# Nine VectorE operations of a graph network's first layer: from one chunk of edges per round to two chunks per two rounds

## The chip, the cores and the metric

The kernel runs on one core of one Trainium2 chip. The metric is the device time of one execution in microseconds, the median of several runs.

## The reference, cut to what matters

Two message-passing layers run over a graph of 3125 nodes with 160 features each (64 scalars and 32 vectors of 3 components) and 100000 edges that are sorted by their target node. The change touches the first layer alone. For every edge:

```python
msg = (rows_src[src] + rows_dst[dst])                 # 160 features: s (64) and v (32 x 3)
w1 = rbf @ W_rbf                                      # 16 -> 224 factors
m1_s = [w_ss*s*y0, w_vv0*(v . y1)/sqrt3]              # 96
m1_v = [w_sv*s*y1, w_vs*v*y0, w_vv1*cross(v,y1)/sqrt2]# 128 x 3
a = leaky(m1_s @ W_alpha) . alpha_dot                 # attention logits, 4 heads
val_s, val_v = m1_s @ Ws_val, (m1_v @ Wv_val) * sigmoid(gate)
m2 = the same tensor product of (sigmoid(val_s), val_v) with y0, y1
h = m2 @ W_vlin                                       # 160 features, stored per edge
```

Later stages take a softmax of the logits over each target's edges, sum the weighted h per target, and run the second layer.

## The kernel before, in words

**Tiling.** The edges are cut into 392 chunks of 256 (`NCH`); a chunk is two tiles (`G` = 2) of 128 edges, an edge to a partition. Four chunks are a super step (`Q`), for which one load brings indices and one the radial features. `loop_steps` writes out the first 8 rounds, then a hardware loop whose body is 8 rounds, then the last ones. A passage from one turn of that body to the next is called a seam below. Every engine runs its own list of rounds t, and semaphores of the table `LA` tie them together.

**One chunk v through the engines.**
- POOL (`gather_src`, line 657) fetches the source and target rows with four indirect DMAs, in the order source, target, source, target, into ring `gat0` (8 chunks, in tile ACC) and ring `dst_rows` (in tile TAB). It waits for `m` and `tp` of chunks 7 or 8 before, that is, until the rings' old contents are used.
- TensorE (`factors0`, line 795) multiplies the radial features into bank W1. ScalarE (`weigh0`, lines 1114 to 1118) scales them by the edge attributes into `WS0`, first half of the chunk at the end of one round, second half at the beginning of the next, and signals `ws`.
- VectorE builds the message. These are the nine operations of the change: `joined0` (line 1484), `products0` (1509), `crossed0` (1515), two in `others0` (1520, 1521), two in `rest_of_s0` (1527, 1528), two in `rest_of_v0` (1534, 1535). The last one signals `m`.
- TensorE turns the message (`t1`, line 803, into bank TR1), ScalarE copies it out (`copies`, line 1129, signals `c1`), TensorE multiplies by the attention and value weights (`e1`, lines 825 and 827, into bank E1, signals `e1`).
- VectorE takes the result: `gated` (1546), `gated_up` (1552), `summed` (1559), `scaled` (1577), `mixed_dots` (1590), `bent_sums` (1566), `mixed_rest` (1597 to 1603, signals `tp`); ScalarE squashes the gates (`squash`, 1140 and 1141) and weighs the rest (`weigh2`, 1152 and 1157).
- TensorE turns this second product (`t2`), ScalarE copies it (`c2`, line 1129), TensorE multiplies by the last weights (`hm`, lines 850 and 852, bank HP). VectorE makes the vector part (`head_products` 1613, `head_values` 1622, signals `hv`), ScalarE copies the scalar part (`scalars0`, 1167), and SyncE stores 256 rows.

**Order within a round.** It is written out by hand in each engine's `stage0`. In VectorE's round t, message operations of chunk t+1 are interleaved with the second half's operations of chunk t-1 and the head operations of chunk t-2, so that no operation reads what the one just before it wrote; `hv` is signalled by the third operation from the end, `m` by the last. TensorE's round is e1(t-1), t2(t-2), t1(t), factors0(t+2), hm(t-2). ScalarE's is the second half of weigh0(t+1), squash(t-1), the copies of t2(t-2) and t1(t), weigh2(t-1), the first half of weigh0(t+2), scalars0(t-2):

```python
weigh0(t + 1, total, 1)
squash(t + -1, total)
copies(t + -2, total, "t2", TR2, MT2, "c2", "h")
copies(t, total, "t1", TR1, MT, "c1", "e1")
weigh2(t + -1, total)
weigh0(t + 2, total, 0)
scalars0(t + -2, total)
```

So ScalarE ends a round by waiting for VectorE's `hv`, and starts the next with the second half of the factors. All data are float32.

Of the kernel before, what the change touches and what calls it, by code (L numbers as in the profile page):

```python
# [8 lines left out]
ALU = mybir.AluOpType  # L9
# [75 lines left out]
class Step:  # L85
# [23 lines left out]

    def quad_past(self, n):  # L110
        return self.base is not None or self.first // Q >= n
# [39 lines left out]
def program(nc, a, out):  # L151
    ctx = ExitStack()
    with ctx:
# [62 lines left out]
        WS0 = flat[:, 2560:2560 + 2 * G * NF].rearrange("p (b g f) -> p b g f", b=2, g=G)  # L216
# [16 lines left out]
        dst_rows = tabf[:, 0:8 * G * D].rearrange("p (b g f) -> p b g f", b=8, g=G)  # L233
        hC = [t[:, 8 * D * i:8 * D * (i + 1)] for t in (scf, tabf) for i in range(2)]
# [151 lines left out]
        def _(sp):  # L386
# [123 lines left out]
            def sp0(t, total):  # L510
                load_places(t + 8, total)
                load_rbf(t + 5, total)
                store(t + -2, total)
# [117 lines left out]
        def _(pool):  # L631
# [11 lines left out]
            def gather_src(v, total):  # L643
                if not inside(v, total):
                    return
                if v.past(7):

                    wait(LA["m"], v.num - 6)
# [94 lines left out]
        def _(pe):  # L743
# [62 lines left out]
            def t1(v, total):  # L806
                if not inside(v, total):
                    return

                pe.wait_ge(LA["m"], v.num + 1)  # L810
                if v.past(1):
                    pe.wait_ge(LA["c1"], v.num)
                turn(M[:, v.par], TR1, LA["t1"])
# [42 lines left out]
            def stage0(t, total):  # L856
# [3 lines left out]
                factors0(t + 2, total)  # L860
                hm(t + -2, total)
            loop_steps(pe, Q, NS, False, 2, 2, stage0)
# [179 lines left out]
        def _(act):  # L1042
# [63 lines left out]
            def weigh0(v, total, g):  # L1106
# [3 lines left out]
                if g == 0:  # L1110
                    act.wait_ge(LA["w"], v.num + 1)
                    if v.past(2):
                        act.wait_ge(LA["m"], v.num - 1)
                    nc.scalar.activation(WS0[:, v.par, :, 96:160], ax(W1[:, 96:97], (224, G), (1, S)), ACT.Copy)
                w, o = W1[:, 224 * g:224 * (g + 1)], WS0[:, v.par, g, :]
# [53 lines left out]
            def stage0(t, total):  # L1169
                weigh0(t + 1, total, 1)  # L1170
# [4 lines left out]
                weigh0(t + 2, total, 0)  # L1175
                scalars0(t + -2, total)
            loop_steps(act, Q, NS, False, 2, 2, stage0)
# [175 lines left out]
        def _(dve):  # L1353
# [123 lines left out]

            def joined0(v, total):
# [3 lines left out]
                dve.wait_ge(LA["ga"][v.slot8], v.slot_round(64, 8))  # L1482
                rows = gat0[:, v.slot8].rearrange("p g f -> p (g f)")
                return ch.count(TT(rows, rows, dst_rows[:, v.slot8].rearrange("p g f -> p (g f)"), ALU.add))

            def products0(v, total, joined):

                if not inside(v, total):
                    return None
                dve.wait_ge(LA["ws"], v.num + 1)  # L1490
                if v.past(1):

                    dve.wait_ge(LA["m"], v.num)
                if v.past(2):

                    dve.wait_ge(LA["t1"], v.num - 1)
                ch.wait(joined)
                Mt = M[:, v.par]

                def feat(lo, *dims):  # L1500
                    return ax(gat0[:, v.slot8, 0, lo:lo + 1], (D, G), *dims)

                def wgt(lo, *dims):
                    return ax(WS0[:, v.par, 0, lo:lo + 1], (NF, G), *dims)

                def mid(lo, *dims):
                    return ax(Mt[:, 0, lo:lo + 1], (MW, G), *dims)

                return mid, feat, wgt, ch.count(TT(mid(0, (C, 3), (1, C)), feat(S, (C, 3), (1, C)), wgt(160, (64, 3), (1, C)),
                                                   ALU.mult))  # L1510

            def crossed0(v, total, parts):
                if parts:
                    mid, feat, wgt, dots = parts
                    TT(fX[:, :, 0:2, 0, :], feat(S, (C, 2), (1, C)), wgt(192 + 64, (64, 2), (1, C)), ALU.mult)

            def others0(v, total, parts):
                if parts:
                    mid, feat, wgt, dots = parts
                    TT(fX[:, :, 0:2, 1, :], feat(S + C, (C, 2), (1, C)), wgt(192, (64, 2), (1, C)), ALU.mult)  # L1520
                    return ch.count(TT(fX[:, :, 2], feat(S + 2 * C, (-2 * C, 2), (1, C)), wgt(192, (128, 2), (1, C)), ALU.mult))

            def rest_of_s0(v, total, parts):
                if parts:
                    mid, feat, wgt, dots = parts
                    ch.wait(dots)
                    TT(mid(C, (1, C)), mid(0, (1, C)), mid(C, (1, C)), ALU.add)
                    TT(mid(96, (S, 2), (1, S)), feat(0, (0, 2), (1, S)), wgt(C, (S, 2), (1, S)), ALU.mult)

            def rest_of_v0(v, total, parts, crosses):  # L1530
                if parts:
                    mid, feat, wgt, dots = parts
                    ch.wait(crosses)
                    TT(mid(96 + P + 96, (C, 3), (1, C)), fX[:, :, :, 0, :], fX[:, :, :, 1, :], ALU.subtract)
                    TT(mid(96 + P, (C, 3), (1, C)), feat(S, (C, 3), (1, C)), wgt(0, (0, 3), (1, C)), ALU.mult)\  # L1535
# [88 lines left out]
            def stage0(t, total):  # L1624
                ch.restart()
                gated(t + -1, total)
                joined = joined0(t + 1, total)
                ups = gated_up(t + -1, total)
                parts = products0(t + 1, total, joined)
                done = summed(t + -1, total, ups)  # L1630
                scaled(t + -1, total, done)
                crossed0(t + 1, total, parts)
# [326 lines left out]
```

## Time and profile before

| what | value |
| --- | --- |
| median of 3 runs | 3856.96 us (3856.09 to 3858.71) |
| the profiled execution's own time | 3859.59 us |
| its span | 3858.0 us |
| TensorE busy | 3505.2 us, 91% of the span |
| VectorE busy | 3548.4 us, 92% |
| ScalarE busy | 3054.7 us, 79% |
| POOL busy | 2579.3 us, 67% |
| TensorE's granted clock, mean | 0.979 |

The profile comes from one execution. Its engines are PE (TensorE), PEld (TensorE's weight load), DVE (VectorE), ACT (ScalarE), POOL (GpSimd) and SP (SyncE). Busy time counts an instruction from its start to its end; VectorE's and ScalarE's instructions overlap their neighbours, so what an instruction costs its engine is the distance from its start to the next one's, and its length is what a reader of its result has to wait. In square brackets a timeline gives the idle time before an instruction and what ended it. The first layer's loop fills the span from about 80 to 2293 us; the softmax and the sums follow until about 2700 us, then comes the second layer.

### The profile page before, as it was taken

To read this page: it belongs to the slowest core of one execution; us is meant where nothing else is said; L and a number is where in the kernel's file an instruction comes from. 1 tells how busy PE (TensorE), PEld (TensorE's weight loads), DVE (VectorE), ACT (ScalarE), POOL (GpSimd) and SP (SyncE) were. 2 spreads that over 40 slices of the span, in tenths; PEclk is the share of its full clock that TensorE was granted. 3 is DMA by queue.
4 is the path that set the end of the run, shared out by engine and by line. 5 is a ranking of instruction groups with operands and counts; after the bars stand their busy time and mean duration, and the time that the engine had idled before them with its cause. 6 is when DMAs were issued, how large, how long until landed. Compare 5 with 4: busy or idle time off the path is not lost. (4 is left out here: it accounts for less than half of the span.)

```text
span 3858.0 us, 97024 instructions
## 1 busy us (share of the span) xinstructions
PE 3505.2 (91%) x21340; PEld 2634.3 (68%) x21340; DVE 3548.4 (92%) x12738; ACT 3054.7 (79%) x11217; POOL 2579.3 (67%) x2474
## 2 busy tenths in 40 slices
PE   4999999999999999999999976995999999999997
PEld 3888888888888888888888865884333333333335
DVE  5999999999999999999999997885999999999995
ACT  4888888888888888888888865774778777787774
POOL 1777777777777777777777720111777777777772
PEclk8999999999999999999999988997999999999999
DMA  4333333333333333333333338992343343334334
GB/s 110 92 94 95 94 92 91 92 91 91 91 91 92 91 90 91 93 91 91 91 91 92 91 113 260 274 254 83 91 95 93 95 96 92 95 95 96 93 95 116
DMA packets 296922, 411.00 MB, mean 107 GB/s; under 512 B 98581, under 2 KB 231573, under 8 KB 296597
## 3 DMA queue, kind: packets, MB, share of 16 engines
q0 software_dynamic: 127568, 211.04, 23.9%
q1 hardware_dynamic: 169284, 199.21, 16.0%
q8 instruction: 23, 0.38, 0.0%
q14 instruction: 47, 0.38, 0.0%
HBM read 309.09 MB, written 100.94 MB: 106 GB/s over the span
## 5 line engine op out<-in xcount | busy, mean ns | idle before, releaser
L657 POOL DMA_INDIRECT ACC<-src_tab,idx x784 | 817.4, 1043 | 330.8 <-issue 221.1
L657 POOL DMA_INDIRECT TAB<-dst_tab,idx x784 | 850.5, 1085 | 245.0 <-issue 152.1
L724 POOL DMA_INDIRECT ACC<-hid_tab,idx x784 | 810.8, 1034 | 245.7 <-issue 243.3
L803 PE MATMUL TR<-ident,M 128*128 128x128 f32 x4704 | 664.3, 277 | 86.6 <-DVE M L1535 73.8
L803 PEld LDWEIGHTS TR<-ident,M 128*128 128x128 f32 x4704 | 520.5, 141 | 180.0 <-DVE M L1535 177.5
L1129 ACT ACTIVATE MT<-TR 128x768 f32<-128x768 f32 x784 | 610.8, 862 | 3.5 <-PE TR L803 3.5
L1118 ACT ACTIVATE ACC<-W,ACC 128x64 f32<-128x64 f32 x2352 | 597.1, 360 | 0.0
L852 PE MATMUL HP<-w_hv,MT 128*128 128x128 f32 x3136 | 520.0, 288 | 0.0
L827 PE MATMUL E<-w_mv,MT 128*128 128x128 f32 x3136 | 477.1, 275 | 0.0
L827 PEld LDWEIGHTS E<-w_mv,MT 128*128 128x128 f32 x3136 | 437.0, 191 | 0.0
L1312 ACT ACTIVATE ACC<-TR,y 128x128 f32<-128x128 f32 (+1 forms) x1568 | 418.6, 553 | 11.4 <-PE TR L987 11.4
L1312 ACT ACTIVATE TAB<-TR,y 128x128 f32<-128x128 f32 (+1 forms) x1568 | 414.1, 424 | 0.0
L852 PEld LDWEIGHTS HP<-w_hv,MT 128*128 128x128 f32 x3136 | 413.2, 192 | 0.0
L795 PE MATMUL W<-w_rbf,rbf 128*128 128x224 f32 x1568 | 381.6, 366 | 20.7 <-DMA rbf<-in_rbf_line 13.7
L1002 PE MATMUL HP<-M,ohE 128*128 128x480 f32 x800 | 375.9, 593 | 24.5 <-DVE M L1866 23.4
L1002 PE MATMUL E<-M,ohE 128*128 128x480 f32 x768 | 360.2, 592 | 17.4 <-DVE M L1866 16.3
L825 PE MATMUL E<-w_ms,MT 128*128 128x168 f32 x1568 | 354.3, 308 | 2.2 <-issue 2.2
L1167 ACT ACTIVATE ACC<-HP 128x128 f32<-128x128 f32 x392 | 108.9, 278 | 294.4 <-DVE ACC L1622 291.2
L987 PEld LDWEIGHTS TR<-w_edge,ACC 64*128 64x128 f32 x1568 | 119.1, 185 | 324.6 <-ACT TAB L1312 157.1
L850 PEld LDWEIGHTS HP<-w_hs,MT 128*128 128x128 f32 x1568 | 235.6, 190 | 122.7 <-ACT MT L1129 122.6
L850 PE MATMUL HP<-w_hs,MT 128*128 128x64 f32 x1568 | 301.1, 274 | 3.1 <-ACT MT L1129 3.1
L1116 ACT ACTIVATE ACC<-W,ACC 128x96 f32<-128x96 f32 x784 | 290.2, 370 | 11.4 <-issue 11.4
(279 smaller groups left out, 7828.3 us busy)
## 6 DMA issues: line engine op xcount, KB each, us to landing
h_tab<-ACC SPq DMA_DIRECT2D x392, 160.0 KB, 2.1
SC<-h_tab SPq DMA_DIRECT2D x50, 640.0 KB, 5.1
TAB<-h_tab SPq DMA_DIRECT2D x48, 640.0 KB, 5.2
ACC<-in_e64T SPq DMA_DIRECT2D x98, 256.0 KB
ACC<-src_tab,idx POOLq DMA_INDIRECT x784
TAB<-dst_tab,idx POOLq DMA_INDIRECT x784
ACC<-hid_tab,idx POOLq DMA_INDIRECT x784, 3.7
agg_tab<-ACC POOLq DMA_DIRECT2D x49, 240.0 KB, 4.1
```

The lines of the kernel that those rows point to most:

```text
L657: pool.indirect_dma_start(tile[:, v.slot8, g, :], None, table.ap(), bass.IndirectOffsetOnAxis(ap=idx[:, v.sslot, c:c + 1], axis=0))\
L724: pool.indirect_dma_start(gat1[:, v.slot8, g, :], None, hid_tab.ap(), bass.IndirectOffsetOnAxis(ap=idx[:, v.sslot, c:c + 1], axis=0))\
L795: ins = nc.tensor.matmul(W1[:, 224 * g:224 * (g + 1)], rbf[:, v.sslot, v.place, g, :], w_rbf[:, :], start=True, stop=True)
L803: ins = nc.tensor.transpose(to[:, b * G + g, :], Mt[:, g, lo:lo + w], ident[:, :])
L825: nc.tensor.matmul(E1[:, 0, ES * g:ES * (g + 1)], MT[:, 0, g, :], w_ms0[:, :], start=True, stop=True)
L827: ins = nc.tensor.matmul(E1[:, 1, P * g:P * (g + 1)], MT[:, 1 + b, g, :], w_mv0[:, b, :], start=(b == 0), stop=(b == 1))
L850: nc.tensor.matmul(HP[:, S * g:S * (g + 1)], MT2[:, 0, g, :], w_hs0[:, :], start=True, stop=True)
L852: ins = nc.tensor.matmul(HP[:, P + P * g:P + P * (g + 1)], MT2[:, 1 + b, g, :], w_hv0[:, b, :], start=(b == 0), stop=(b == 1))
L1002: ins = nc.tensor.matmul(AG[v.sslot][:, 0:MW], ohE[:, v.slot, g, :], M[:, v.par, g, :], start=(v.place == 0 and g == 0), stop=(v.place == ...
L1118: ins = nc.scalar.activation(o[:, 160 + 64 * k:224 + 64 * k], w[:, 160:224], ACT.Copy, scale=y_at(v, g, 1 + k))
L1129: nc.scalar.activation(dst[:, 0:3].rearrange("p k g e -> p (k g e)"), tr[:, 0:3 * G, :].rearrange("p a e -> p (a e)"), ACT.Copy).then_inc( ...
L1312: ins = nc.scalar.activation(WS[v.slot][:, g, P * k:P * k + hi - lo], wg_[:, lo:hi], ACT.Copy, scale=y1[:, v.sslot, c:c + 1])
```

## The change

The nine message operations work on two chunks (four tiles) at a time. VectorE's rounds alternate. `first_of_pair` (even t) has `joined0`, `products0`, `crossed0` and the first of `others0` for chunks t+2 and t+3. `second_of_pair` (odd t) has the last cross product, the two operations of `rest_of_s0`, the subtraction and the last product for chunks t+1 and t+2. Semaphore `m` counts pairs. The message tile has four places (`M4`, in tile SC, which is free in this stage) in place of two, its scratch `fX4` is twice as long, and `WS0` has four places, two in ACC and two in TAB. The factors (`factors0`, `weigh0`) run two chunks further ahead, and the load of radial features two rounds earlier. `head_values` is now the last operation of both kinds of round. Everything computed is the same.

The diff, cut; of `joined0` to `rest_of_v0` only the new lines are shown, the old ones stand above:

```diff
+    @property
+    def pair(self):
...
+        return self.first // 2 if self.base is None else self.base * (self.q // 2) + self.first // 2
...
     def quad_past(self, n):
...
-        WS0 = flat[:, 2560:2560 + 2 * G * NF].rearrange("p (b g f) -> p b g f", b=2, g=G)
...
+        WS0 = [t[:, 2560:2560 + 2 * G * NF].rearrange("p (b g f) -> p b g f", b=2, g=G) for t in (flat, tabf)]
+        M4 = scf[:, 0:4 * G * MW].rearrange("p (b g f) -> p b g f", b=4, g=G)
+        fX4 = scf[:, 4 * G * MW:4 * G * MW + 2 * G * 6 * C].rearrange("p (g k s c) -> p g k s c", g=2 * G, k=3, s=2)
...
             def sp0(t, total):
...
-                load_rbf(t + 5, total)
+                load_rbf(t + 7, total)
...
             def gather_src(v, total):
...
-                if v.past(7):
...
-                    wait(LA["m"], v.num - 6)
+                if v.past(8):
...
+                    wait(LA["m"], v.pair - 3)
...
-                pe.wait_ge(LA["m"], v.num + 1)
+                pe.wait_ge(LA["m"], v.pair + 1)
...
-                turn(M[:, v.par], TR1, LA["t1"])
+                turn(M4[:, v.slot], TR1, LA["t1"])
...
             def e1(v, total):
...
-                factors0(t + 2, total)
+                factors0(t + 4, total)
...
-            loop_steps(pe, Q, NS, False, 2, 2, stage0)
+            loop_steps(pe, Q, NS, False, 4, 2, stage0)
...
-                    if v.past(2):
-                        act.wait_ge(LA["m"], v.num - 1)
-                    nc.scalar.activation(WS0[:, v.par, :, 96:160], ax(W1[:, 96:97], (224, G), (1, S)), ACT.Copy)
-                w, o = W1[:, 224 * g:224 * (g + 1)], WS0[:, v.par, g, :]
+                    if v.past(4):
+                        act.wait_ge(LA["m"], v.pair - 1)
+                    nc.scalar.activation(WS0[v.slot // 2][:, v.par, :, 96:160], ax(W1[:, 96:97], (224, G), (1, S)), ACT.Copy)
+                w, o = W1[:, 224 * g:224 * (g + 1)], WS0[v.slot // 2][:, v.par, g, :]
...
             def stage0(t, total):
-                weigh0(t + 1, total, 1)
+                weigh0(t + 3, total, 1)
...
-                weigh0(t + 2, total, 0)
+                weigh0(t + 4, total, 0)
...
-            loop_steps(act, Q, NS, False, 2, 2, stage0)
+            loop_steps(act, Q, NS, False, 4, 2, stage0)
...
+            def feat(v, lo, *dims):
+                return ax(gat0[:, v.slot8, 0, lo:lo + 1], (D, 2 * G), *dims)
...
+            def wgt(v, lo, *dims):
+                return ax(WS0[v.slot // 2][:, 0, 0, lo:lo + 1], (NF, 2 * G), *dims)
...
+            def mid(v, lo, *dims):
+                return ax(M4[:, v.slot, 0, lo:lo + 1], (MW, 2 * G), *dims)
...
             def joined0(v, total):
...
+                for u in (v, v + 1):
+                    dve.wait_ge(LA["ga"][u.slot8], u.slot_round(64, 8))
+                rows = gat0[:, v.slot8:v.slot8 + 2].rearrange("p b g f -> p (b g f)")
+                return ch.count(TT(rows, rows, dst_rows[:, v.slot8:v.slot8 + 2].rearrange("p b g f -> p (b g f)"), ALU.add))
...
             def products0(v, total, joined):
...
+                    return
+                dve.wait_ge(LA["ws"], v.num + 2)
...
+                    dve.wait_ge(LA["m"], v.pair)
+                if v.past(4):
...
+                    dve.wait_ge(LA["t1"], v.num - 2)
...
+                TT(mid(v, 0, (C, 3), (1, C)), feat(v, S, (C, 3), (1, C)), wgt(v, 160, (64, 3), (1, C)), ALU.mult)
...
+            def crossed0(v, total):
+                if inside(v, total):
+                    TT(fX4[:, :, 0:2, 0, :], feat(v, S, (C, 2), (1, C)), wgt(v, 192 + 64, (64, 2), (1, C)), ALU.mult)
...
+            def others0(v, total):
+                if inside(v, total):
+                    ch.count(TT(fX4[:, :, 0:2, 1, :], feat(v, S + C, (C, 2), (1, C)), wgt(v, 192, (64, 2), (1, C)), ALU.mult))
...
+            def last_cross0(v, total):
+                if inside(v, total):
+                    return ch.count(TT(fX4[:, :, 2], feat(v, S + 2 * C, (-2 * C, 2), (1, C)), wgt(v, 192, (128, 2), (1, C)), ALU.mult))
...
+            def rest_of_s0(v, total):
+                if inside(v, total):
+                    TT(mid(v, C, (1, C)), mid(v, 0, (1, C)), mid(v, C, (1, C)), ALU.add)
+                    TT(mid(v, 96, (S, 2), (1, S)), feat(v, 0, (0, 2), (1, S)), wgt(v, C, (S, 2), (1, S)), ALU.mult)
...
+            def cross_sums0(v, total, crosses):
+                if inside(v, total):
...
+                    TT(mid(v, 96 + P + 96, (C, 3), (1, C)), fX4[:, :, :, 0, :], fX4[:, :, :, 1, :], ALU.subtract)
...
+            def rest_of_v0(v, total):
+                if inside(v, total):
+                    TT(mid(v, 96 + P, (C, 3), (1, C)), feat(v, S, (C, 3), (1, C)), wgt(v, 0, (0, 3), (1, C)), ALU.mult)\
...
-            def stage0(t, total):
+            def first_of_pair(t, total):
...
-                joined = joined0(t + 1, total)
+                joined = joined0(t + 2, total)
...
-                parts = products0(t + 1, total, joined)
+                products0(t + 2, total, joined)
...
-                crossed0(t + 1, total, parts)
+                crossed0(t + 2, total)
...
-                crosses = others0(t + 1, total, parts)
-                rest_of_s0(t + 1, total, parts)
+                others0(t + 2, total)
...
-                rest_of_v0(t + 1, total, parts, crosses)
-            loop_steps(dve, Q, NS, False, 1, 2, stage0)
...
+            def second_of_pair(t, total):
...
+                ch.restart()
+                gated(t + -1, total)
+                crosses = last_cross0(t + 1, total)
+                ups = gated_up(t + -1, total)
+                rest_of_s0(t + 1, total)
+                done = summed(t + -1, total, ups)
+                scaled(t + -1, total, done)
+                cross_sums0(t + 1, total, crosses)
+                dots = mixed_dots(t + -1, total)
+                bent_sums(t + -1, total)
+                mixed_rest(t + -1, total, dots)
+                up = head_products(t + -2, total)
+                rest_of_v0(t + 1, total)
+                head_values(t + -2, total, up)
...
+            def stage0(t, total):
+                (second_of_pair if t.par else first_of_pair)(t, total)
+            loop_steps(dve, Q, NS, False, 2, 2, stage0)
```

**VectorE, from the end of a round into the next.** Before (la is the scratch of the logits, svy, vals and V those of the values, tG that of the head; a_hv and the like are the semaphores of `LA`):

```order
L1613 TENSOR_TENSOR tG<-HP,ACC 128x192 [waits a_hv,a_h]
L1520 TENSOR_TENSOR fX<-ACC 128x2x2x32
L1521 TENSOR_TENSOR fX<-ACC 128x2x64
L1527 TENSOR_TENSOR M<-M 128x2x32 [waits s_dve]
L1528 TENSOR_TENSOR M<-ACC 128x2x128
L1622 TENSOR_TENSOR ACC<-HP,tG 128x2x96 [waits s_dve,a_st0]
L1534 TENSOR_TENSOR M<-fX 128x2x96 [waits s_dve]
L1535 TENSOR_TENSOR M<-ACC 128x2x96
L81 ISA [waits s_dve]
L1546 SCALAR_TENSOR_TENSOR la<-E,adot 128x144 [waits a_tp,a_e1]
L1484 TENSOR_TENSOR ACC<-ACC,TAB 128x320 [waits a_ga0]
L1552 TENSOR_TENSOR svy<-E,ACC 128x192
```

The same place of the change, where a second round ends and a first one begins:

```order
L1619 TENSOR_TENSOR tG<-HP,ACC 128x192 [waits a_hv,a_h]
L1541 TENSOR_TENSOR SC<-ACC,TAB 128x4x96
L1628 TENSOR_TENSOR ACC<-HP,tG 128x2x96 [waits s_dve]
L81 ISA [waits s_dve]
L1552 SCALAR_TENSOR_TENSOR la<-E,adot 128x144 [waits a_tp,a_e1]
L1501 TENSOR_TENSOR ACC<-ACC,TAB 128x640 [waits a_ga1,a_ga0]
L1558 TENSOR_TENSOR svy<-E,ACC 128x192
L1515 TENSOR_TENSOR SC<-ACC 128x4x96 [waits a_t1,s_dve,a_m,a_ws]
L1565 TENSOR_TENSOR vals<-E,svy 128x192 [waits s_dve]
```

The operation that signals `hv` (L1622, now L1628) had two message operations behind it in its round and now has none. The joining addition covers 640 elements in place of 320 and waits for two gather slots.

**VectorE, the beginning of a second round in the change:**

```order
L1552 SCALAR_TENSOR_TENSOR la<-E,adot 128x144 [waits a_tp,a_e1]
L1527 TENSOR_TENSOR SC<-ACC 128x4x64
L1558 TENSOR_TENSOR svy<-E,ACC 128x192
L1531 TENSOR_TENSOR SC<-SC 128x4x32
L1532 TENSOR_TENSOR SC<-ACC 128x4x128
L1565 TENSOR_TENSOR vals<-E,svy 128x192 [waits s_dve]
L1583 TENSOR_TENSOR V<-gate,vals 128x192 [waits s_dve,a_m2a,a_sg]
L1537 TENSOR_TENSOR SC<-SC 128x4x96 [waits s_dve]
```

This round has no joining addition and waits for no gather; five of the nine paired operations stand in it, four in the first.

## Rows read from the trace of the kernel before

**Rows 1.** The page: busy time of each engine
```profile
PE 3505.2 (91%) x21340; PEld 2634.3 (68%) x21340; DVE 3548.4 (92%) x12738; ACT 3054.7 (79%) x11217; POOL 2579.3 (67%) x2474
```

**Rows 2.** Windows: 1000 us of the first layer; busy us and (instructions) per engine, clock, DMA
```profile
1000.00:2000.00 1000.00, 961.20 (x7147) 855.60 (x7146) 969.23 (x3931) 863.47 (x3217) 768.54 (x715) 1.00 0.34 91
```

**Rows 3.** Timeline of VectorE, one round: start us, length us, line, tiles, shapes
```profile
999.40 0.30 DVE L1546 SCALAR_TENSOR_TENSOR la<-E,adot 128x144 f32<-128x144 f32 x1
999.62 0.48 DVE L1484 TENSOR_TENSOR ACC<-ACC,TAB 128x320 f32<-128x320 f32 x1
1000.02 0.35 DVE L1552 TENSOR_TENSOR svy<-E,ACC 128x192 f32<-128x192 f32 x1
...
1003.80 0.41 DVE L1528 TENSOR_TENSOR M<-ACC 128x256 f32<-128x256 f32 x1
1004.14 0.34 DVE L1622 TENSOR_TENSOR ACC<-HP,tG 128x192 f32<-128x192 f32 x1
...
1004.94 0.29 DVE L1546 SCALAR_TENSOR_TENSOR la<-E,adot 128x144 f32<-128x144 f32 x1
```

**Rows 4.** Groups by line and shape, VectorE, 100 to 2600 us
```profile
L1750 DVE TENSOR_TENSOR ACC<-SC,ex 128x768 f32<-128x768 f32 x49 | 46.6, 951 | 0.0
```

**Rows 5.** Timeline of ScalarE from the end of that round
```profile
1004.52 0.28 ACT L1167 ACTIVATE ACC<-HP 128x128 f32<-128x128 f32 x1 [0.72 <-DVE ACC L1622]
1004.69 0.34 ACT L1116 ACTIVATE ACC<-W,ACC 128x96 f32<-128x96 f32 x1
1004.91 0.73 ACT L1118 ACTIVATE ACC<-W,ACC 128x64 f32<-128x64 f32 x3
1005.50 0.25 ACT L1140 ACTIVATE gate<-E 128x64 f32<-128x64 f32 x1
...
1005.77 1.56 ACT L1129 ACTIVATE MT<-TR 128x768 f32<-128x768 f32 x2
```

**Rows 6.** The page: group of the PSUM copies
```profile
L1129 ACT ACTIVATE MT<-TR 128x768 f32<-128x768 f32 x784 | 610.8, 862 | 3.5 <-PE TR L803 3.5
```

**Rows 7.** Timeline of TensorE, the same round
```profile
1005.07 0.87 PE L803 MATMUL TR<-ident,M 128*128 128x128 f32 x6 [0.21 <-DVE M L1535]
...
1006.68 0.43 PE L850 MATMUL HP<-w_hs,MT 128*128 128x64 f32 x2
...
1008.12 0.45 PE L825 MATMUL E<-w_ms,MT 128*128 128x168 f32 x2
...
1009.14 0.61 PE L827 MATMUL E<-w_mv,MT 128*128 128x128 f32 x4
```

**Rows 8.** Timeline of TensorE, start of the first layer
```profile
94.27 0.97 PE L827 MATMUL E<-w_mv,MT 128*128 128x128 f32 x4
```

**Rows 9.** Timeline of VectorE, start and end of the first layer
```profile
95.28 0.31 DVE L1546 SCALAR_TENSOR_TENSOR la<-E,adot 128x144 f32<-128x144 f32 x1 [0.77 <-PE E L827]
96.98 0.49 DVE L1484 TENSOR_TENSOR ACC<-ACC,TAB 128x320 f32<-128x320 f32 x1 [1.40 <-DMA TAB<-dst_tab,idx]
...
107.78 0.29 DVE L1546 SCALAR_TENSOR_TENSOR la<-E,adot 128x144 f32<-128x144 f32 x1
...
2281.09 0.30 DVE L1546 SCALAR_TENSOR_TENSOR la<-E,adot 128x144 f32<-128x144 f32 x1
```

**Rows 10.** Windows: POOL's gathers (line 657), first 479 us of them
```profile
80.00:559.00 479.00, 368.90 (x361) 0.98 0.35 93
```

**Rows 11.** Timeline of POOL: at the start, in the steady part, at a seam
```profile
94.42 0.95 POOL L657 DMA_INDIRECT TAB<-dst_tab,idx  x1 [0.30 <-issue]
...
109.61 0.98 POOL L657 DMA_INDIRECT TAB<-dst_tab,idx  x1 [0.30 <-issue]
...
1005.34 1.12 POOL L657 DMA_INDIRECT TAB<-dst_tab,idx  x1 [0.30 <-DVE M L1535]
1006.76 0.98 POOL L657 DMA_INDIRECT ACC<-src_tab,idx  x1 [0.30 <-issue]
...
1037.59 1.17 POOL L657 DMA_INDIRECT ACC<-src_tab,idx  x1 [0.78 <-DVE M L1603]
```

More of the change, by code:

```diff
@@ L1481, in joined0 @@
                     return None
-                dve.wait_ge(LA["ga"][v.slot8], v.slot_round(64, 8))
-                rows = gat0[:, v.slot8].rearrange("p g f -> p (g f)")
-                return ch.count(TT(rows, rows, dst_rows[:, v.slot8].rearrange("p g f -> p (g f)"), ALU.add))
+                for u in (v, v + 1):
+                    dve.wait_ge(LA["ga"][u.slot8], u.slot_round(64, 8))
+                rows = gat0[:, v.slot8:v.slot8 + 2].rearrange("p b g f -> p (b g f)")
+                return ch.count(TT(rows, rows, dst_rows[:, v.slot8:v.slot8 + 2].rearrange("p b g f -> p (b g f)"), ALU.add))
@@ L1486, in products0 @@
             def products0(v, total, joined):
                 if not inside(v, total):
[L1489 to L1493, printed above, removed]
+                    return
+                dve.wait_ge(LA["ws"], v.num + 2)
                 if v.past(2):
-                    dve.wait_ge(LA["t1"], v.num - 1)
+                    dve.wait_ge(LA["m"], v.pair)
+                if v.past(4):
+                    dve.wait_ge(LA["t1"], v.num - 2)
@@ L1497, in products0 @@
                 ch.wait(joined)
[L1498 to L1532, printed above, removed]
+                TT(mid(v, 0, (C, 3), (1, C)), feat(v, S, (C, 3), (1, C)), wgt(v, 160, (64, 3), (1, C)), ALU.mult)
@@ L1533, in rest_of_v0 @@
+            def rest_of_s0(v, total):
[4 more added lines that the diff above has]
+                if inside(v, total):
                     ch.wait(crosses)
-                    TT(mid(96 + P + 96, (C, 3), (1, C)), fX[:, :, :, 0, :], fX[:, :, :, 1, :], ALU.subtract)
@@ L1535, in rest_of_v0 @@
-                    TT(mid(96 + P, (C, 3), (1, C)), feat(S, (C, 3), (1, C)), wgt(0, (0, 3), (1, C)), ALU.mult)\
+                    TT(mid(v, 96 + P + 96, (C, 3), (1, C)), fX4[:, :, :, 0, :], fX4[:, :, :, 1, :], ALU.subtract)
+            def rest_of_v0(v, total):
+                if inside(v, total):
+                    TT(mid(v, 96 + P, (C, 3), (1, C)), feat(v, S, (C, 3), (1, C)), wgt(v, 0, (0, 3), (1, C)), ALU.mult)\
                         .then_inc(LA["m"], 1)
```

## The prediction

> **What bounds the kernel now.** I read the page's busy times first: VectorE and TensorE stand at 92% and 91% of the span, so neither can be dismissed [rows 1]. Then the windows: in 1000 us from the middle of the first layer VectorE is busy for 969, TensorE for 961, ScalarE for 863, POOL for 769, at a granted clock of 1.00 [rows 2]. Busy shares don't decide here, so I went to the timelines of one round. VectorE's round starts at 999.40 and the next at 1004.94, 5.54 us later, and hardly anything in it waits [rows 3]. TensorE, in contrast, stands idle for 0.21 us until VectorE's last message operation [rows 7], and ScalarE for 0.72 us until VectorE's `hv` [rows 5]. So VectorE sets the pace. From the round that starts at 107.78 to the one at 2281.09 there are 389 rounds: 5.587 us each [rows 9], that is 5.54 and about 0.05 for the seams of the loop, once in 8 rounds.
>
> **The change, part by part.**
>
> *VectorE's own work.* From start to start an operation of 320 elements takes 0.40 us, one of 192 takes 0.26, one of 256 takes 0.34 [rows 3]. That is 0.067 us for each operation and 1.04 ns for each element. It holds for long ones too: 768 elements last 951 ns against 0.48 us for 320, 1.05 ns an element [rows 3, 4]. The nine operations of a chunk have 1600 elements (320, 192, 3 x 128, 64, 256, 2 x 192): 1.67 + 9 x 0.067 = 2.27 us. For two chunks at once they cost 3.33 + 0.60 = 3.93, or 1.97 a chunk. The saving is 0.30 us a chunk, and VectorE's round falls from 5.54 to 5.24. A first round has 1.87 us of them (640, 384, 256, 256 elements), a second 2.07 (256, 128, 512, 384, 384); what remains of a round is 5.54 - 2.27 = 3.27. So the rounds last 5.14 and 5.34, 10.48 for two.
>
> *The chain from `hv` to the next but one round.* This is what I expect to be late next. `head_values` ends at 1004.48 [rows 3]. ScalarE starts its scalar copy at 1004.52, then the second half of the factors, then the gates, and at 1005.77 the copy of TR2 [rows 5], which takes 0.86 [rows 6] and so ends at 1006.63. TensorE's `hm` starts at 1006.68, `e1` at 1008.12, the last four matmuls of it at 1009.14 for 0.61 us, to 1009.75 [rows 7]. `gated` needs that result. At the start of the layer it waited for just this and began 0.04 us after it, 95.28 after 94.27 + 0.97 [rows 8, 9]. So the earliest start is 1009.80, 5.32 us after `hv`; in fact it starts at 1004.94 + 5.54 = 1010.48, with 0.68 to spare. Now `hv` moves: it had 0.46 us of the round left behind it, and is now signalled 0.08 after the round is over, since its operation is the last, starts 0.27 before the end and lasts 0.35. From the start of a second round to the start of the second round after it there are then at least 5.34 + 0.08 + 5.32 = 10.74 us, where VectorE's own work is 10.48. Hence 5.37 a chunk. With the seams as before, 0.05, that is 5.42. Half of VectorE's gain is kept as time, the rest becomes a wait of `gated` for TensorE.
>
> *TensorE and ScalarE* do the same instructions. TensorE's round has 0.21 us of waiting for `m` and a little before `hm`, so some 5.2 of work, under 5.37. ScalarE has 4.8. `m` comes once for two rounds and somewhat before a round's end; the turns of every other chunk don't wait for it. The weights `ws` of two chunks must be there for the first round's product: they are ready some 1.25 us into it, the product stands at 1.22 and then waits 0.1 or 0.2, in a round that has that slack in the chain above. I count nothing.
>
> *SyncE* loads the radial features two rounds earlier, 98 loads that nobody waited for, at nothing. The cover is three rounds; without it TensorE would wait once in four rounds, by the nearest row for the 1.6 us that a gather takes to land [rows 9, 11], 0.4 a chunk.
>
> *POOL.* The gathers are the same, 4 a chunk. At the start one takes 0.95 us and 0.30 to the next, 1.25 in all [rows 11]; over the first 479 us there are 361 of them, 1.327 each [rows 10], so 5.31 a chunk; in the steady part most are 1.41 apart (1005.34 to 1006.76), where POOL is kept back by VectorE, as its wait of 0.78 at a seam shows [rows 11]. Their wait for `m` by pairs is not the later one, `tp` is. Free-running, POOL has 5.31 against the 5.42 needed: the margin is 2%, and I add 0.01 for it. Forecast 5.43.
>
> *The start.* VectorE's first rounds run at the pace of the gathers. Before, a round joined one chunk, and the round of 107.78 (t = 3) was the first not to wait. In the change the round t = 2 joins chunks 4 and 5, for which the 24th gather must land. It starts at 109.61 and lasts 0.98 [rows 11]; the twelfth, from 94.42, ended at 95.37 and let `joined0` go at 96.98, 1.6 later [rows 9, 11]. So the joining starts at 112.2, its round at about 112.0, and t = 3 at 117.1: 9.3 us later than before. Nothing gives this back at the other end, where the last rounds have no message operations in either version.
>
> *Sum.* 389 x (5.587 - 5.43) = 61.1, less 9.3: 51.8 us. The profiled execution took 3859.6, so 3807.8. The median of the runs is 2.6 lower: **3805 us**. All other stages stay.
>
> **A rule that speaks against it.** The gathers lengthen from 0.95 to 1.12 us while VectorE is saturated [rows 11]. The Trainium skill, SBUF — State Buffer, "Who interferes with whom", says that a VectorE instruction with two SBUF inputs contends with a GpSimd instruction that reads SBUF, and that the pair is held for the whole instruction. By this rule longer operations would hold the gathers up longer; the second rival below gives what that would cost.
>
> **The rivals.**
> 1. *The chain doesn't bind*, because TensorE's modelled ends are late or ScalarE's part shrinks. Then the round is 5.24 + 0.05 = 5.29: 389 x 0.297 - 9.3 = 106 us, 3751. For it: all slack is in tenths of a microsecond. Against it: each link is a start that follows the end before it by 0.04 or 0.05.
 For operations with both inputs in SBUF I get 0.98 over 2 x 5.54, 0.09 us (with 1.25 that is 1.34, close to 1.327), and 2.64 over 2 x 10.74, 0.12, with the change. Then 0.034 x 4 = 0.14 more a chunk, 5.45: 389 x 0.137 - 9.3 = 44, 3813. If the delay grows faster, to 1.38 a gather, it is 5.52 and 3840. VectorE would show waits at the joining addition.
> 3. *The gathers bind harder, and it is slower.* All four at the 1.41 that stands in the steady part give 5.64 a chunk: 389 x 0.053 + 9.3 = 30 us lost, 3887. It decides from 1.39 a gather, where 4 x 1.39 = 5.56 saves only the 9.3 us of the start. For it: VectorE's longest operation in the loop grows from 0.40 to 0.73. Against it: in the free part, with VectorE as full, the mean was 1.327, and VectorE waiting for gathers leaves them more room.
>
> **How the numbers follow.** Forecast (3790 to 3820) 0.48; rival 1, 0.14; rival 2, 0.23; between 2 and 3, within 0.2% of before (about 8 us, what a measurement of this kernel can tell from no change), 0.06; rival 3, 0.09. Rival 2 up to 3849 counts as faster, so faster 0.85, same 0.06, slower 0.09. The range reaches from between the forecast and rival 1, 3765 (all that is beyond it is the better part of rival 1), to the upper end of rival 2, 3849.
>
> **What the profile would show.** Right: pairs of rounds of 10.8 us; `gated` (now line 1552) of second rounds idle 0.2 to 0.3 us until TensorE's E; the joining addition 0.81 us long and with hardly a wait; ScalarE's wait before its scalar copy smaller than 0.72; `t1` waiting every other round at most; the round t = 3 at about 117. Rival 1: no wait at line 1552 and rounds of 5.24. Rivals 2 and 3: waits at line 1501 for the gathers, and a mean gather over 1.35 from start to start. Wrong altogether: paired operations that cost more than 0.067 us and 1.04 ns an element, or a wait of the first product for `ws` well over 0.2 us.

## The result, and the profile after

| | median of runs, us | runs | ratio to before, 95% interval |
|---|---|---|---|
| before | 3857.70 | 6 (3856.09 to 3859.07) | |
| the change | 3992.93 | 6 (3988.55 to 3995.40) | 1.0349 [1.0336, 1.0363] |

The change makes the kernel 135 us slower. The forecast was 3805 us, faster; neither it nor the range (3765 to 3849) holds the time, and none of the three rivals is what happened.

The page of the changed kernel, whose profiled execution took 3988.55 us at a mean granted clock of 0.959 (before 0.979): busy times, then three of the costliest groups.

```profile
span 3986.9 us, 95767 instructions
...
PE 3548.7 (89%) x21340; PEld 2718.8 (68%) x21340; DVE 3475.1 (87%) x10974; ACT 3062.8 (77%) x11217; POOL 2476.7 (62%) x2474
...
L664 POOL DMA_INDIRECT ACC<-src_tab,idx x784 | 759.0, 968 | 574.0 <-DVE M L1609 326.7
...
L802 PE MATMUL W<-w_rbf,rbf 128*128 128x224 f32 x1568 | 404.6, 381 | 189.8 <-ACT TAB L1125 130.4
L859 PE MATMUL HP<-w_hv,MT 128*128 128x128 f32 x3136 | 554.2, 302 | 0.0
```

Against [rows 1] VectorE is busy for 73 us less, as intended, but the others wait more: TensorE's matmuls of the factors (L802) stand 130 us for ScalarE, and POOL, before its source gathers, stands 327 us for VectorE. So the gathers are not what holds the kernel up.

First a pair of rounds in the middle (VectorE and ScalarE, some rows):

```profile
1011.94 0.30 DVE L1552 SCALAR_TENSOR_TENSOR la<-E,adot 128x144 f32<-128x144 f32 x1
...
1012.16 0.82 DVE L1501 TENSOR_TENSOR ACC<-ACC,TAB 128x640 f32<-128x640 f32 x1
...
1013.41 0.56 DVE L1515 TENSOR_TENSOR SC<-ACC 128x384 f32<-128x384 f32 x1 [0.16 <-DVE svy L1558]
...
1017.07 0.35 DVE L1628 TENSOR_TENSOR ACC<-HP,tG 128x192 f32<-128x192 f32 x1
...
1017.43 0.31 DVE L1552 SCALAR_TENSOR_TENSOR la<-E,adot 128x144 f32<-128x144 f32 x1
...
1022.83 0.29 DVE L1552 SCALAR_TENSOR_TENSOR la<-E,adot 128x144 f32<-128x144 f32 x1
```

The pair takes 10.89 us, 5.44 a chunk; before it was 5.54 [rows 3]. Inside the loop the change works. Now a seam of the loop, once in 8 rounds, all engines (some rows):

```profile
997.15 0.28 ACT L1174 ACTIVATE ACC<-HP 128x128 f32<-128x128 f32 x1 [0.58 <-DVE ACC L1628]
...
997.37 0.31 DVE L1552 SCALAR_TENSOR_TENSOR la<-E,adot 128x144 f32<-128x144 f32 x1 [0.25 <-DVE tG L1619]
...
999.86 0.34 ACT L1123 ACTIVATE TAB<-W,ACC 128x96 f32<-128x96 f32 x1 [2.43 <-issue]
...
1000.87 1.02 PE L802 MATMUL W<-w_rbf,rbf 128*128 128x224 f32 x4 [2.58 <-ACT TAB L1125]
...
1001.05 0.56 DVE L1515 TENSOR_TENSOR SC<-ACC,TAB 128x384 f32<-128x384 f32 x1 [2.38 <-ACT TAB L1125]
...
1003.11 1.17 PE L859 MATMUL HP<-w_hv,MT 128*128 128x128 f32 x4
...
1004.99 0.98 POOL L664 DMA_INDIRECT ACC<-src_tab,idx  x1 [3.26 <-DVE M L1609]
...
1006.60 0.31 DVE L1552 SCALAR_TENSOR_TENSOR la<-E,adot 128x144 f32<-128x144 f32 x1 [1.19 <-PE E L834]
```

This round lasts from 997.37 to 1006.60, 9.23 us. ScalarE, which had just made its scalar copy, stands still for 2.43 us with the releaser "issue": nothing that the profile shows held it. The weights of the next pair come late, VectorE's first product waits 2.38 us for them, and then `gated` 1.19 more for TensorE. TensorE is late for two reasons: it stood idle for 2.58 us, and behind that its granted clock was lower:

```profile
1003.50:1006.60 3.10, 3.10 (x18) 3.10 (x18) 1.66 (x8) 2.07 (x10) 1.31 (x2) 0.62 0.00 0
1011.94:1022.83 10.89, 10.36 (x79) 9.27 (x78) 10.45 (x37) 9.64 (x36) 7.98 (x9) 1.00 0.31 84
```

The windows (columns as in [rows 2]) show a granted clock of 0.62 behind the pause, on average between the two levels of 1.2 and 2.4 GHz, and 1.00 (2.4 GHz) in the pair further on; four matmuls of L859 take 1.17 us at the first and 0.66 at the second. From the start of the factors (L802) to the end of E (L834) TensorE takes 5.69 us here (1000.87 to 1006.56) and 4.05 in the pair further on (1013.24 to 1017.29). The waits of ScalarE over the layer say how often it stands still (us in total, times, longest):

```profile
ACT ACC L1174 <- DVE ACC L1628: 300.1, 392, 2.5
ACT TAB L1123 <- issue: 116.6, 46, 2.8
```

The loop runs 47 times and so returns 46 times: 46 pauses of 2.5 us. Before, the same place had 0.25 us:

```profile
1032.81 0.34 ACT L1116 ACTIVATE ACC<-W,ACC 128x96 f32<-128x96 f32 x1 [0.25 <-issue]
```

One more line of the page differs, the queue that brings instructions, before:

```profile
q14 instruction: 47, 0.38, 0.0%
```

and after:

```profile
q14 instruction: 275, 2.25, 0.2%
```

228 packets of 8.2 KB more, 5 a return.

From t = 3 to t = 392 there are 389 rounds: before from 107.78 to 2285.67, 5.599 each; after from 118.29 to 2420.64, 5.919 each. That is 124.5 us lost in the loop and 10.5 at the start, 135.0 in all. The medians differ by 135.2, but that it fits so well is partly luck: the two profiled spans, from which the 135.0 comes, differ by only 128.9, because the stages behind the loop took 6 us less in the change's (1566.3 against 1572.3). Nothing here explains those 6 us.

### The profile page after: what moved, and what is told of

Read it like the earlier page. It is cut to its first block and busy times, and to the rows that moved or that the text cites. A ratio compares the mean times of both kernels' runs of the same rounds, so it can differ in the third digit from the quotient of the medians.

```text
span 3986.9 us, 95767 instructions
## 1 busy us (share of the span) xinstructions
PE 3548.7 (89%) x21340; PEld 2718.8 (68%) x21340; DVE 3475.1 (87%) x10974; ACT 3062.8 (77%) x11217; POOL 2476.7 (62%) x2474
## 5 line engine op out<-in xcount | busy, mean ns | idle before, releaser
L664 POOL DMA_INDIRECT ACC<-src_tab,idx x784 | 759.0, 968 | 574.0 <-DVE M L1609 326.7
L664 POOL DMA_INDIRECT TAB<-dst_tab,idx x784 | 809.4, 1032 | 239.0 <-issue 234.8
L802 PE MATMUL W<-w_rbf,rbf 128*128 128x224 f32 x1568 | 404.6, 381 | 189.8 <-ACT TAB L1125 130.4
L859 PE MATMUL HP<-w_hv,MT 128*128 128x128 f32 x3136 | 554.2, 302 | 0.0
L834 PE MATMUL E<-w_mv,MT 128*128 128x128 f32 x3136 | 492.1, 281 | 0.0
L834 PEld LDWEIGHTS E<-w_mv,MT 128*128 128x128 f32 x3136 | 456.0, 198 | 0.0
L802 PEld LDWEIGHTS W<-w_rbf,rbf 128*128 128x128 f32 x1568 | 269.2, 192 | 272.6 <-ACT TAB L1125 167.4
L859 PEld LDWEIGHTS HP<-w_hv,MT 128*128 128x128 f32 x3136 | 441.4, 203 | 0.0
L810 PE MATMUL TR<-ident,SC 128*128 128x128 f32 x2352 | 321.8, 273 | 3.2 <-DVE SC L1541 3.2
L810 PE MATMUL TR<-ident,M 128*128 128x128 f32 x2352 | 321.6, 273 | 0.2 <-issue 0.2
L1125 ACT ACTIVATE TAB<-W,ACC 128x64 f32<-128x64 f32 x1176 | 298.4, 359 | 0.0
```

Of the source, the lines that this page charges most:

```text
L664: pool.indirect_dma_start(tile[:, v.slot8, g, :], None, table.ap(), bass.IndirectOffsetOnAxis(ap=idx[:, v.sslot, c:c + 1], axis=0))\
L802: ins = nc.tensor.matmul(W1[:, 224 * g:224 * (g + 1)], rbf[:, v.sslot, v.place, g, :], w_rbf[:, :], start=True, stop=True)
L810: ins = nc.tensor.transpose(to[:, b * G + g, :], Mt[:, g, lo:lo + w], ident[:, :])
L834: ins = nc.tensor.matmul(E1[:, 1, P * g:P * (g + 1)], MT[:, 1 + b, g, :], w_mv0[:, b, :], start=(b == 0), stop=(b == 1))
L859: ins = nc.tensor.matmul(HP[:, P + P * g:P + P * (g + 1)], MT2[:, 1 + b, g, :], w_hv0[:, b, :], start=(b == 0), stop=(b == 1))
L1125: ins = nc.scalar.activation(o[:, 160 + 64 * k:224 + 64 * k], w[:, 160:224], ACT.Copy, scale=y_at(v, g, 1 + k))
```

## The experiments

**Theory P (place).** ScalarE's loop body is 286 instructions before and 292 in the change, and it starts behind 282 and 300 instructions of its program: the longer lead writes out two more rounds ahead of the loop. The hypothesis: if instructions come in blocks of 256 and an engine holds two, a body over two blocks is never fetched again, and one that touches three must be fetched at every return. Its rival: the pairing itself (the later `hv`, the wait for two chunks' weights) makes the seam long.

The first tool is idle instructions on ScalarE, ahead of its loop and outside it. They raise a semaphore that nothing waits for:

```diff
+            for _ in range(60):
+                act.sem_inc(s_passed, 1)
             act.wait_ge(s_y, 16)
```

*a_pad60*: the change with 60 of them (later lines of the kernel have numbers higher by 2). Expected:

> The changed kernel with 60 idle semaphore instructions ahead of ScalarE's first-layer loop, so that the loop's 292 instructions start at the 360th of the stream in place of the 300th. Theory P (place): the 2.4 to 2.8 us in which ScalarE stands still at each of the 47 seams come from fetching the loop's instructions anew, which depends on where in the stream the body lies. By the Trainium skill, Runtime: NRT & Kernel Launch, 'Instruction fetch mechanics', a taken branch stalls when its target isn't in the current window of two blocks of 256 instructions. By P the bubbles go, ScalarE's idle time of 116.6 us before the factors' copy falls to under 15, the fetch queue's 275 packets fall to about 47, the granted clock returns to 0.98, and the time is 3818 (3808 to 3830): rounds of 5.47 in place of 5.60, less 10 us at the start. Theory L (length): 292 instructions are too many wherever they lie; then 3993 as before. Theory D: the factors' lead of four chunks, or their place in tile TAB, stops ScalarE at the seam; then 3993 too.

Measured: 3819.38 us, ratio 0.9903 [0.9888, 0.9918], clock 0.976, 47 packets on the queue for instructions. (One of its five executions took 10563 us, which nothing explains; the median without it is 3818.5, and the ratio leaves it out.) Sixty instructions that do nothing take 174 us off the change (172 by the ratios), and theories L and D fall. ScalarE's 46 pauses shrink to those of before:

```profile
ACT TAB L1125 <- issue: 10.8, 46, 0.3
```

*b_pad24*: the kernel before with 24 of them. Expected:

> The kernel before with 24 idle semaphore instructions ahead of ScalarE's loop; nothing else. Its body of 286 instructions starts at the 306th in place of the 282nd and ends where the changed kernel's ends. Theory P: it gets the bubble too, 2.4 us of ScalarE at each of 47 seams and some 1.2 us more by TensorE's lower clock after it, 3.6 x 47 = 170, so 4010 to 4040, with about 275 fetch packets. Theory L (286 instructions are few enough) and theory D (nothing of the change is in it): 3858, 47 packets.

Measured: 4060.84 us, ratio 1.0533 [1.0517, 1.0549], 276 packets: 21 us above the range expected, in the direction expected. The old kernel, with not one operation of the pairing, falls into the same hole (ScalarE's waits from 80 to 2260 us):

```profile
ACT ACC L1118 <- issue: 107.1, 43, 2.7
ACT MT L1131 <- issue: 33.6, 43, 1.1
```

Here ScalarE stops twice at nearly every return.

*a_pad256*: the change with 256. Expected:

> The changed kernel with 256 idle semaphore instructions ahead of ScalarE's loop. Theory P with blocks of 256: the body lies in its blocks as in the changed kernel, and the bubble is as large, 3985 to 4005. If the place counts but not in steps of 256, or if any padding helps (by the time it lets pass), it is fast, near 3820 to 3835. L and D: 3993.

Measured, in two executions: 3984.31 us, ratio 1.0335 [1.0316, 1.0354], 277 packets. A whole block of idle instructions leaves the time as it was by the ratios (1.0335 and 1.0349, intervals that overlap), so what counts is the position modulo 256, not the presence of idle instructions or the delay that they bring.

*b_lead*: the kernel before with one half of the change alone, the longer lead.

```diff
-                weigh0(t + 1, total, 1)
+                weigh0(t + 3, total, 1)
...
-                weigh0(t + 2, total, 0)
+                weigh0(t + 4, total, 0)
...
-            loop_steps(act, Q, NS, False, 2, 2, stage0)
+            loop_steps(act, Q, NS, False, 4, 2, stage0)
```

Likewise on TensorE and SyncE, and with four places of `WS0`. Expected:

> The kernel before with one half of the change alone: factors two chunks further ahead on TensorE and ScalarE, loads of features two rounds earlier, four buffers of weights; VectorE works on one chunk at a time as before. ScalarE's loop body then has 292 instructions and starts at the same place of its program as in the change. Theory P (place): about 4055 us (4035 to 4075), over 250 packets on the instruction fetch queue, ScalarE still for over 2 us once in 8 rounds. Rival (the pairing on VectorE has a part in the loss at the seams): between 3850 and 3950.

Measured: 4012.83 us, ratio 1.0412 [1.0394, 1.0429], 276 packets: 22 us below the range expected, but far above that of the rival. The pause is the same (ScalarE's waits, the same stretch):

```profile
ACT TAB L1116 <- issue: 108.1, 44, 2.7
```

*b_lead_pad60*: the same with 60 idle instructions. Expected:

> The same with 60 idle instructions ahead of ScalarE's loop. Theory P: the time of before, 3857 within 6 us, since VectorE's round of 5.54 us is untouched and nothing waited for the factors; about 47 fetch packets. If the longer lead costs or brings something by itself (buffers, ScalarE's six more instructions), it shows here as a difference from before.

Measured: 3850.64 us, ratio 0.9989 [0.9980, 0.9999], 48 packets. These two settle the blame: the loss came in with the lead, by where it puts the loop and by its six instructions more in the body. The pairing has at most a small part in it: a return costs 3.5 us without it and 3.8 with it. As work the lead costs nothing.

*a_pad10* and *a_pad40*: the change with 10 and 40, around the boundary. Expected, in this order:

> The change with 10 idle instructions ahead of ScalarE's loop: its body then still lies over three blocks of 256 by theory P, so the time is that of the change, 3985 to 4000 us, with over 250 fetch packets. A rival in which any few idle instructions cure it (timing at the entry of the loop) gives 3819.

> The change with 40 idle instructions: by theory P the body starts behind a block boundary and lies over two blocks; 3819 us within 5, 47 fetch packets.

Measured, in two executions each: 4074.76 us, ratio 1.0572 [1.0551, 1.0593], 275 packets; and 3822.87, 0.9918 [0.9898, 0.9938], 46 packets. The side of the boundary was right both times, but a_pad10 did not take the time of the change, as had been expected: it is 82 us slower. It stops twice (the same view):

```profile
ACT TAB L1125 <- issue: 104.1, 42, 2.7
ACT gate L1149 <- issue: 47.5, 42, 1.5
```

The runs bound the place of the boundary. A body of 286 is over three blocks if a boundary lies less than 30 behind its start, one of 292 if less than 36. Start 306 with 286 is slow, and start 340 with 292 is fast; start 282 with 286 is fast. So a boundary lies between the 312th and the 336th of ScalarE's instructions.

The second stops narrow this down. The last operation before the stop and the one behind it, in b_pad24 and in a_pad10:

```profile
1023.36 0.30 ACT L1143 ACTIVATE M<-E 128x128 f32<-128x128 f32 x1
1024.73 1.51 ACT L1131 ACTIVATE MT<-TR 128x768 f32<-128x768 f32 x2 [1.06 <-issue]
```

```profile
1032.56 0.71 ACT L1127 ACTIVATE TAB<-W,ACC 128x64 f32<-128x64 f32 x3
1034.43 0.22 ACT L1149 ACTIVATE gate<-E 128x64 f32<-128x64 f32 x1 [1.16 <-issue]
```

Counted in the built programs, b_pad24 has run 14 of the instructions of its body and stops at one of the next three, a_pad10 has run 9 and stops at one of the next four. With the starts of 306 and 310 that is a place 320 to 322 and 319 to 322 instructions into the program: the same one in both, and inside the bounds. If these stops are at the boundary, the change and b_lead (300) run some 20 instructions before they reach it, b_pad24 (306) about 15 and a_pad10 (310) about 11. The loss a return, against the nearest kernel without pauses, grows as that stretch gets shorter: 162.2 / 46 = 3.5 us (b_lead), 173.5 / 46 = 3.8 (the change), 205.7 / 46 = 4.5 (b_pad24), 251.9 / 46 = 5.5 (a_pad10). That the next block isn't there either when a short stretch has run out, and that this is the second stop, fits these places but is argued, not shown.

The Trainium skill, "Runtime: NRT & Kernel Launch", section "Instruction fetch mechanics", describes this: blocks of 256 instructions, two of them held, sequential prefetch, and "A taken branch whose target isn't in the current 2-page window forces a DMA fetch of the target page before execution can continue". The nine kernels with and without pauses agree with its 256 and its two blocks (by themselves they would allow blocks of 128, three of them held, as well); it gives no price, and here that is 2.4 to 2.8 us of one engine and 3.5 to 5.5 of the kernel.

**With the seam cured, what bounds the pair?** a_pad60's pairs take 10.92 us (the median over the layer; for one, VectorE's `gated` at 1159.02, 1164.42, 1169.95), where the prediction has 10.48 of VectorE's own work and 10.74 by the chain from `hv`. Theory C said the chain binds.

*a_pad60_hv*: `hv` earlier in second rounds, with the last subtraction of `mixed_rest` moved behind `head_products`:

```diff
...
-                mixed_rest(t + -1, total, dots)
+                crosses2 = mixed_rest(t + -1, total, dots, split=True)
                 up = head_products(t + -2, total)
+                mixed_last(t + -1, total, crosses2)
+                head_values(t + -2, total, up)
                 rest_of_v0(t + 1, total)
-                head_values(t + -2, total, up)
```

Expected:

> The changed kernel with the 60 instructions, and in VectorE's second rounds the head's product and sum stand on either side of the last subtraction of the second product, so that hv is signalled ahead of the last message product, 0.47 us before the end of the round in place of 0.08 after it (0.27 of that by the one place earlier). Theory C (the chain hv, factors, gates, copy, two groups of matmuls, gated limits the pair of rounds): the bound from second rounds goes from 10.74 to under 10.3, the one from first rounds, 5.14 + 0.08 + 5.32 = 10.54, is left; a pair takes 10.54 to 10.6 in place of 10.8, and the time is 25 to 40 us under that of the padded kernel. Rival G (the gathers limit it) or V (VectorE's own 10.48 and its self-waits): within 8 us of the padded kernel.

Measured: 3812.81 us, ratio 0.9880 [0.9864, 0.9897]. Only 6.6 us better than a_pad60 where theory C had 25 to 40, so the chain alone was not what held it. A new wait stood in the trace, at the joining addition, and POOL ran without pause (VectorE's waits from 120 to 2200 us):

```profile
DVE ACC L1503 <- DMA TAB<-dst_tab,idx: 38.6, 101, 1.1
```

From this I made two theories for the next runs: V, VectorE's own waits set the pace; G, the gathers do, at 1.37 us from start to start (their length 1.06 and 0.30 between).

*a_pad60_prod*: in first rounds the first product stands behind `summed`.

```diff
+                done = summed(t + -1, total, ups)
                 products0(t + 2, total, joined)
-                done = summed(t + -1, total, ups)
```

Expected:

> As a_pad60 (the change, 60 idle instructions ahead of ScalarE's loop), and in the first round of a pair the first product of the pair stands behind the sum (vals) instead of ahead of it: it then no longer stands 0.16 us for the weights, and fills the 0.13 us in which V waits for vals. Theory V (VectorE's own waits set the pace): 0.16 to 0.2 us less a pair of 10.92, about 30 us below a_pad60, near 3788. Theory G (a gather from start to start takes 1.36 us where POOL never waits, as in a_pad60_hv, 5.46 a chunk): at most 8 us below a_pad60, 3808 to 3818, with the joining addition waiting for gathers and POOL no longer waiting for VectorE's last subtraction.

Measured: 3801.56 us on a chip where the kernel before took 3867.36, ratio 0.9832 [0.9815, 0.9848]; on the scale of the others (3857) that is 3792, so about 27 us better than a_pad60. V was right in size; G was right only in that POOL no longer waits for VectorE's last subtraction. The product no longer waits, the joining addition doesn't either, and in its place stands the wait that the prediction had named (VectorE's waits from 120 to 2200 us, then two rows of the timeline with the end of the round between them):

```profile
DVE la L1554 <- PE E L834: 42.8, 191, 0.3
```

```profile
1153.46 0.30 DVE L1554 SCALAR_TENSOR_TENSOR la<-E,adot 128x144 f32<-128x144 f32 x1
...
1158.20 0.61 PE L834 MATMUL E<-w_mv,MT 128*128 128x128 f32 x4
...
1158.29 0.35 DVE L1630 TENSOR_TENSOR ACC<-HP,tG 128x192 f32<-128x192 f32 x1
...
1158.84 0.31 DVE L1554 SCALAR_TENSOR_TENSOR la<-E,adot 128x144 f32<-128x144 f32 x1 [0.21 <-PE E L834]
...
1164.23 0.30 DVE L1554 SCALAR_TENSOR_TENSOR la<-E,adot 128x144 f32<-128x144 f32 x1
```

TensorE's E ends at 1158.81 and `gated` starts at 1158.84. The pair takes 10.77 us; the chain from `hv` was forecast to give 10.74.

*a_pad60_prod_hv*: both edits. Expected:

> Both edits, hv earlier and the product later. Theory V: 3770 to 3785. Theory G: the time of a_pad60_hv, 3812 within 5, since POOL is free-running there already; more waiting at the joining addition.

Measured: 3749.25 us beside 3867.36, ratio 0.9698 [0.9680, 0.9717]; on the scale of 3857 it is 3741. Better than either theory said (V at least 3770), and G, as a fixed pace of the gathers, falls. The rounds alternate between 5.36 and 5.18, 10.54 a pair against VectorE's own 10.48, and VectorE hardly waits for anything (982.67 us busy in 1000):

```profile
1000.00:2000.00 1000.00, 981.09 (x7564) 908.60 (x7563) 982.67 (x3308) 915.24 (x3405) 769.85 (x756) 1.00 0.34 96
```

One thing stays open. Behind 120 us POOL stands no longer than 0.3 us between two gathers in this run, as everywhere, so it doesn't wait for VectorE, and VectorE doesn't wait for it. Yet their distance doesn't change: the last gather that a pair needs ends at 417.96 and the joining addition starts at 419.76, and 140 pairs later it is 1899.80 and 1901.60, 1.80 us both times. Two independent paces would drift apart. So the time that a gather takes and VectorE's rounds are coupled, and the runs don't show which leads; that VectorE's own work is the limit of this version is therefore likely, not shown.

So the same move of `hv` yields 6.6 us with the product in its old place, where the gathers become late, and 1.4% or 52 us with the product moved, where the chain was the limit. This version beats both kernels: 3% under the one before, 6% under the change.

## Why the prediction was wrong

**The step that failed** is "With the seams as before, 0.05, that is 5.42", which rests on "*TensorE and ScalarE* do the same instructions". The instructions that compute are the same, but ScalarE's loop grew by 6 instructions and moved by 18, and came to lie over three blocks. In the change a chunk takes 5.92 us on average and 5.44 away from the seams, so the seams cost 0.47 a chunk in place of 0.05. By the timeline a seam's round is 3.8 us too long (9.23 for 5.44), 46 times: 174, more than the whole gain. I had read the seams as a constant and so had no rival in which a seam changes. The group [rows 11] showed a seam only by POOL's wait of 0.78; the pause of 0.25 on ScalarE at each return stood in the trace of before and was not read, nor was the body's length of 286 counted.

**The other steps, held against a_pad60**, the change without the pauses:

- *The count.* From 107.78 to 2281.09 there are 388 rounds, not 389, so before took 5.60 a round, not 5.587. It hardly matters: the seams' share was taken from the same count and would have been 0.06, the forecast for a round 5.44, and the saving only 1 us larger.
- *VectorE's own work*, right. The paired operations take, from start to start, what 0.067 us and 1.04 ns an element give: 640 elements 0.73 us, 384 elements 0.47, 512 elements 0.60; and the pair of a_pad60_prod_hv, nearly without waits, takes 10.54 for 10.48.
- *The chain*, right as a mechanism and in size, 10.74 forecast and 10.77 measured, but only once the product was out of the way. In the change it is not the last to bind.
- *The waits of VectorE itself*, the term that was mis-sized: "the product ... waits 0.1 or 0.2, in a round that has that slack in the chain". The slack was 10.74 - 10.48 = 0.26 a pair, and the waits are more than that: the first product starts 0.50 us behind `svy` in place of 0.27 (0.23; the 0.16 of the row is what is left behind the end of `svy`), `gated` of a second round 0.36 behind `hv` in place of 0.27 (0.09), and 0.12 is left for small ones. With 10.48 that is 10.92, and the chain lies just under it: in a_pad60 TensorE's E is there at 1169.76 and `gated` starts at 1169.95. So the pair costs 0.18 more than the 10.74 forecast, 0.09 a chunk. Where the 0.09 behind `hv` comes from (perhaps `restart`, which waits for `others0`) was not tried.
- *The start*, right: t = 3 at 117.1 forecast, 118.29 in the change, 117.62 in a_pad60, so 9.8 lost for 9.3.
- *The gathers* (rivals 2 and 3), refuted in the change: in the first 479 us of the layer a_pad60 has 362 gathers where before had 361 [rows 10], and there they last no longer (means 1010 and 1015 ns for the source and target rows; before 1029 and 1019). By the rule of the Trainium skill, SBUF — State Buffer, "Who interferes with whom", longer operations of VectorE would hold them up longer; the free part of the layer doesn't show it. They bind in a_pad60_hv, at 1.37 us from start to start; in a_pad60_prod_hv, with VectorE still fuller, they take 1.32. Their pace depends on the order of VectorE's operations, by 3%, and how is open.

The sum with the measured terms: 389 x (5.599 - 5.482) - 9.8 = 35.7 us, for a_pad60, whose median lies 35.8 under the one of before on its chip (a fit that is better than the few us by which the stages behind the loop vary); then 174 back for the pauses gives 138 lost, where 135 were measured. So without the pauses the change would have been faster, by 36 us where 52 were forecast: right in sign, within the range.

## What to carry to other kernels

Count the instructions of every engine's loop body, and where it starts: a body somewhat longer than a block of 256 (here 286 and 292, on ScalarE) runs free or pays 3.5 to 5.5 us at every return, depending on its position, and any edit ahead of it or in it can flip that. The sign in the profile is a pause with the releaser "issue" at one place of the loop, beside a count of packets for instructions that grows with the number of returns; the cure is idle instructions ahead of the loop, enough to carry its start over the boundary (here 40 or 60; 10 made it worse). And where two limits lie within 2% of each other, take both away before judging either: each alone gave 7 and 27 us, both together 79.

## What was not expected of the hardware

- A loop over three blocks of instructions costs ScalarE 2.4 to 2.8 us at each return, and with few instructions before the boundary a second stop of about 1 us (1.5 at most). The clock adds to it: TensorE, idle for 2.6 us, was granted 0.62 in the 3.1 us shown and took 1.6 us longer for the same matmuls, and the kernel lost 3.8 us a return for a pause of 2.5.
- 24 idle instructions made the tuned kernel before 206 us slower (5.3%). A tuned time can rest on the luck of a position.
- Gathers on POOL and operations on VectorE kept the same distance over 140 pairs of chunks though neither waited for the other (a_pad60_prod_hv); from start to start a gather took 1.32 to 1.37 us with the order of VectorE's operations alone.
